# The normalised y of a gated scan block is transposed by DMA instead of TensorE, and its scale and shift go into the gate's weights

## What is computed

```python
y = scan(...)                                        # (B, L, 512)
mu = y.mean(-1, keepdims=True)
var = ((y - mu) ** 2).mean(-1, keepdims=True)
y = (y - mu) * rsqrt(var + LN_EPS) * ln_gamma + ln_beta
gate = sigmoid(y @ W_gate.T + b_gate)
y = gate * y
return concatenate([silu(z0) * x0, y], axis=-1) @ W_out.T
```

## Time and profile before

| what | value |
|---|---|
| time, median of 3 runs (lowest) | 1279.17 us (1274.94) |
| profiled execution: its time, its span | 1281.52 us, 1279.6 us |
| TensorE busy | 1154.4 us (90%) |
| VectorE busy | 994.8 us (78%) |
| ScalarE busy | 960.4 us (75%) |
| GpSimd busy | 393.4 us (31%) |
| mean granted TensorE clock | 0.961 of full speed |
| hardware DMA queue | 32.1% of 16 engines' span |

### The profile page before, as it was taken

One profiled execution on the slowest core, in us unless ns is written; L12 is line 12 of the kernel. 1 busy time (PEld: TensorE's weight loads), 2 busy tenths in 40 slices (PEclk: granted clock), 3 DMA queues, 4 the chain that ended last, 5 costly groups with the idle time before them and its releaser, 6 DMA issues.

```text
span 1279.6 us, 22535 instructions
## 1 busy us (share of the span) xinstructions
PE 1154.4 (90%) x8534; PEld 736.7 (58%) x8534; DVE 994.8 (78%) x1958; ACT 960.4 (75%) x1662; POOL 393.4 (31%) x500
## 2 busy tenths in 40 slices
PE   4577889999999999999999999999998999989885
PEld 1354565647575665657575666656565574747453
DVE  5889786878978798979888897979787696666443
ACT  5847466787979797887879797887877867676744
POOL 1112314152423324142524324252522314232420
PEclk9878899999999999999999999999998999999896
DMA  4720103242423433242423333232253203222443
GB/s 138 202 64 9 34 10 67 34 108 41 94 59 71 80 56 95 42 100 51 92 51 87 71 67 76 51 92 57 52 99 72 54 18 75 50 67 50 82 83 82
DMA packets 238971, 89.10 MB, mean 70 GB/s; under 512 B 207760, under 2 KB 235152, under 8 KB 238864
## 3 DMA queue, kind: packets, MB, share of 16 engines
q1 hardware_dynamic: 238864, 87.67, 32.1%
HBM read 24.32 MB, written 8.39 MB: 26 GB/s over the span
## 4 chain that ended last, share of the span: by engine, by line
PE 59%; ACT 17%; DVE 13%; DMA 5%; issue 4%; POOL 2%; SPq 0%; ACTq 0%; DVEq 0%
PE bank L166 29%; PE bank L140 29%; ACT h L141 3%; ACT L161 3%; DMA hT<-hb 2%; DVE cv L144 2%; DVE EM L144 2%; DVE hb L142 2%; ACT yT L141 2%; ACT hb L141 2%; ACT cv L141 2%; ACT yhl L141 1%; DVE tg L144 1%; POOL caty L142 1%; DVE hn L144 1%
## 5 line engine op out<-in xcount | busy, mean ns | idle before, releaser
L166 PE MATMUL bank<-xnT,win 128*128 128x512 f16 (+1 forms) x1040 | 264.7, 386 | 23.4 <-DMA xnT<-hb 19.1
L144 DVE SCALAR_TENSOR_TENSOR cv<-bank,cws,cv 128x510 f32<-128x510 f32 (+5 forms) x240 | 178.3, 744 | 13.5 <-ACT cv L141 3.0
L166 PE MATMUL bank<-yhl,wg 128*128 128x512 f16 x704 | 169.5, 391 | 10.8 <-DVE yhl L142 10.8
L166 PEld LDWEIGHTS bank<-xnT,win 128*128 128x128 f16 (+1 forms) x1040 | 100.2, 102 | 133.3 <-issue 30.6
L140 PE MATMUL bank<-wpj,hT 128*128 128x256 f16 x1040 | 133.8, 285 | 26.5 <-DMA hT<-hb 23.9
L140 PE MATMUL bank<-wfc,x3T 128*128 128x512 f16 x512 | 132.6, 387 | 8.4 <-DVE dec L145 3.6
L161 ACT ACT_TABLE_LOAD x105 | 134.7, 1283 | 1.9
L140 PEld LDWEIGHTS bank<-wpj,hT 128*128 128x128 f16 x1040 | 103.7, 102 | 53.6 <-ACT hb L141 12.2
L141 ACT ACTIVATE h<-bank,rs 128x512 f32<-128x512 f32 x128 | 87.4, 683 | 62.2 <-PE bank L140 61.2
L166 PEld LDWEIGHTS bank<-yhl,wg 128*128 128x128 f16 x704 | 69.8, 100 | 99.3 <-issue 13.7
L142 POOL TENSOR_TENSOR caty<-tg,caty 128x512 f16<-128x512 f32 x64 | 82.6, 1291 | 114.2 <-ACT caty L141 114.2
(11 more groups left out here) (137 smaller groups left out, 2298.5 us busy)
## 6 DMA issues: line engine op xcount, KB each, us to landing
x<-in_x SPq DMA_DIRECT2D x32, 512.0 KB, 4.2
out_y<-x SPq DMA_DIRECT2D x15, 512.0 KB, 3.0
crep<-cv SPq DMA_DIRECT2D x128, 32.0 KB, 2.0
hT<-hb SPq DMA_TRANSPOSE x128, 3.2
segR<-segL SPq DMA_DIRECT2D x64, 6.0 KB
caty<-in_wg SPq DMA_DIRECT2D x1, 1024.0 KB, 6.0
x<-in_wout SPq DMA_DIRECT2D x1, 1024.0 KB, 9.3
hT<-in_wfc SPq DMA_DIRECT2D x1, 1024.0 KB, 11.4
```

Source lines behind the costliest of these rows:

```text
L144: "scalar_tensor_tensor": lambda e: e.scalar_tensor_tensor(*args, **kw),
L166: self.queue.append(lambda e: e.matmul(*args, **kw))
```

## The change

The task `yout` ends after the normalised chunks are written. A new task `yturn` takes over: for each pair of chunks, `hilo_T` splits the normalised y (tokens on partitions) into hi and lo in the stage `hb0`, and DMA transposes write `yhl` with features on partitions (two per pair, four per block). `yhl` is laid out by chunk. Then for each of the four feature groups POOL adds hi and lo into `yf`, and ACT applies gamma and beta in place. The gate's matmuls read the transposed values without gamma and beta: at the start of the program gamma is multiplied into the gate's weights (four pairs of instructions in place of one), and beta times the weights goes into the gate's bias (16 matmuls of one column). The table PLAN has new figures for all tasks, one more row, and EPS is 0.2.

```diff
--- before.py
+++ after.py
@@ -27,39 +27,39 @@
...
-    "yout": (29.7, 29.6, 47.0, 75.6, 76.1, 75.3, 74.2, 63.8, 65.9, 65.6, 67.1, 68.6, 70.8, 74.1, 74.8, 82.6,
...
+    "yturn": (80.5, 80.2, 80.1, 80.8, 90.7, 90.1, 90.8, 91.9, 94.7, 95.3, 95.6, 96.8, 97.6, 99.9, 98.2, 99.8),
...
-EPS = 0.1
+EPS = 0.2
@@ -217,6 +217,7 @@
         s_k2 = sem("s_k2")
         s_ht = [[sem(f"s_ht{n}{q}") for q in range(2)] for n in range(2)]
         s_xt = [sem(f"s_xt{q}") for q in range(2)]
+        s_y = [sem(f"s_y{q}") for q in range(2)]
         s_x3 = [sem(f"s_x3{q}") for q in range(2)]
         s_seg = [sem(f"s_seg{n}") for n in range(2)]
 
@@ -241,6 +242,7 @@
         lnwb = sb("lnwb", [P, 1024])
         aneg = sb("aneg", [P, 8])
         bgh = sb("bgh", [P, 4])
+        lg64 = sb("lg64", [P, 4])
         cws = sb("cws", [P, 5, 4])
         gam = sb("gam", [P, 4])
         mhalf = sb("mhalf", [P, NCH])
@@ -265,7 +267,7 @@
         ec = sb("ec", [P, T])
         dec = sb("dec", [P, NCH])
         yT = sb("yT", [P, 4, T])
-        yhl = sb("yhl", [P, 2, 4, T], f16)
+        yhl = sb("yhl", [P, 2, NCH, 4, P], f16)
         th = sb("th", [P, T])
         yf = yT
         crest = th[:, 0:P]
@@ -374,7 +376,7 @@
         t_ul = V.do([tu], "tensor_copy", ul[:, :, :], ulf)
         t_cw = V.do([ts], "tensor_scalar", cws[:, :, :], sm("cw").rearrange("p (j k) -> p j k", j=5), 1.0 / SW, None,
                     ALU.mult)
-        t_bg = V.do([ts], "tensor_scalar", bgh[:, :], sm("bg"), 0.5, None, ALU.mult)
+        t_lg = V.do([ts], "tensor_scalar", lg64[:, :], sm("lng"), SW, None, ALU.mult)
 
         def rsqrt(waits, dst, var):
             v = V.do(waits, "tensor_scalar", dst, var, 1e-5, None, ALU.add)
@@ -413,11 +415,24 @@
                     dn["an", 0] = V.do([a], "tensor_scalar", aneg[:, :], aneg[:, :], -1.0, None, ALU.mult)
 
         def prep_gate():
-            yield Need(A, ("twg", 0))
-            a1 = A.do([dn["twg", 0]], "activation", wg[:, 0, :, :], wgs, ACT.Copy, scale=SW)
-            dn["wg", 0] = V.do([a1], "scalar_tensor_tensor", wg[:, 1, :, :].rearrange("p k n -> p (k n)"),
-                               wgs.rearrange("p k n -> p (k n)"), SW, wg[:, 0, :, :].rearrange("p k n -> p (k n)"),
-                               ALU.mult, ALU.subtract)
+
+            yield Need(PE, ("twg", 0), banks=1)
+            b, f = take()
+            PE.wait(f, dn["twg", 0], ts)
+            for g in range(4):
+                for k in range(4):
+                    m = PE.do([], "matmul", b[:, g:g + 1], wgs[:, k, g * P:(g + 1) * P], sm("lnb")[:, k:k + 1],
+                              start=(k == 0), stop=(k == 3))
+            v = V.do([m], "tensor_tensor", bgh[:, :], b[:, 0:4], sm("bg"), ALU.add)
+            give(b, v)
+            dn["bg", 0] = V.do([v], "tensor_scalar", bgh[:, :], bgh[:, :], 0.5, None, ALU.mult)
+            for k in range(4):
+                yield Need(A, ("twg", 0))
+                a1 = A.do([dn["twg", 0], t_lg], "activation", wg[:, 0, k, :], wgs[:, k, :], ACT.Identity,
+                          scale=lg64[:, k:k + 1])
+                v = V.do([a1], "scalar_tensor_tensor", wg[:, 1, k, :], wgs[:, k, :], lg64[:, k:k + 1],
+                         wg[:, 0, k, :], ALU.mult, ALU.subtract)
+            dn["wg", 0] = v
 
         def prep_out():
             for half, s in ((0, SW), (1, SW / 2)):
@@ -492,18 +507,20 @@
                     m = PE.do([], "matmul", b_ap, lhs(p, k), rhs(q, k), start=False, stop=True)
             return m
 
-        def hilo_T(a_waits, src, dst, sems, count, done, war, own=0):
+        def hilo_T(a_waits, src, dst, sems, count, done, war, own=0, grid=None):
 
             stage, hb0, hb1, lock = halves[own], ("hb_free0", own), ("hb_free1", own), f"hb{own}"
             yield Need(A, *a_waits, hb0, *war, lock=lock)
             locked.add(lock)
             ready = [old(*k) for k in war]
-            a = A.do([dn[k] for k in a_waits] + [dn[hb0]], "activation", stage[:, 0, :], src, ACT.Copy)
+            hi, lo = (stage[:, q, :].rearrange("p (c k t) -> p c k t", c=grid[0], k=grid[1]) if grid else stage[:, q, :]
+                      for q in range(2))
+            a = A.do([dn[k] for k in a_waits] + [dn[hb0]], "activation", hi, src, ACT.Copy)
             dn["hb", done] = a
             yield Need(SP, ("hb", done))
             t_hi = SP.dma([a] + ready, sems[0], 16 * count, dst[0], stage[:, 0, :], transpose=True)
             yield Need(V, ("hb", done), hb1)
-            v = V.do([a, dn[hb1]], "tensor_tensor", stage[:, 1, :], src, stage[:, 0, :], ALU.subtract)
+            v = V.do([a, dn[hb1]], "tensor_tensor", lo, src, hi, ALU.subtract)
             dn["split", done] = v
             dn[hb0] = [t_hi, v]
             yield Need(SP, ("split", done))
@@ -836,39 +853,39 @@
                                     b[:, :].rearrange("p (j t) -> p j t", j=4), ACT.Identity, scale=rsy[:, c:c + 1],
                                     bias=nmy[:, c:c + 1])
                 give(b, dn["yn", at])
+
+        def yturn(i):
+
+            for p in range(2):
+                yield from hilo_T([("yn", 4 * i + 2 * p), ("yn", 4 * i + 2 * p + 1)],
+                                  yT[:, :, 2 * p * P:2 * p * P + 2 * P].rearrange("p j (c t) -> p c j t", c=2),
+                                  [yhl[:, q, 2 * p:2 * p + 2, :, :].rearrange("p c k t -> p (c k) t") for q in range(2)],
+                                  s_y, 2 * i + p + 1, ("yhl", 2 * i + p), [("gate_read", i - 1)], grid=(2, 4))
+            dn["y", i] = [dn["yhl", 2 * i], dn["yhl", 2 * i + 1]]
             for j in range(4):
-                yield Need(PE, ("yn", 4 * i + 3), ("gate_read", i - 1), banks=1)
-                b, f = take()
-                PE.wait(f, dn["yn", 4 * i + 3])
-                for c in range(NCH):
-                    m = PE.do([], "transpose", b[:, c * P:(c + 1) * P], yT[:, j, chunk(c)], ident)
-                dn["yt_mm", 4 * i + j] = m
-                yield Need(A, ("yt_mm", 4 * i + j))
-                a = A.do([m], "activation", yf[:, j, :], b[:, :], ACT.Identity,
-                         scale=sm("lng")[:, j:j + 1], bias=sm("lnb")[:, j:j + 1])
-                give(b, a)
-                a = A.do([a, old("gate_read", i - 1)], "activation", yhl[:, 0, j, :], yf[:, j, :], ACT.Copy)
-                dn["yhi", 4 * i + j] = a
-                yield Need(V, ("yhi", 4 * i + j))
-                v = V.do([a, old("gate_read", i - 1)], "tensor_tensor", yhl[:, 1, j, :], yf[:, j, :], yhl[:, 0, j, :],
-                         ALU.subtract)
-            dn["y", i] = v
+                yield Need(G, ("y", i))
+                v = G.do([dn["y", i], dn["split", ("yhl", 2 * i + 1)]], "tensor_tensor",
+                         yf[:, j, :].rearrange("p (c t) -> p c t", c=NCH), yhl[:, 0, :, j, :], yhl[:, 1, :, j, :], ALU.add)
+                dn["ysum", 4 * i + j] = v
+                yield Need(A, ("ysum", 4 * i + j))
+                dn["yf", 4 * i + j] = A.do([v], "activation", yf[:, j, :], yf[:, j, :], ACT.Identity,
+                                           scale=sm("lng")[:, j:j + 1], bias=sm("lnb")[:, j:j + 1])
 
         def gate(i):
             for g in range(4):
                 at = 4 * i + g
                 yield Need(PE, ("y", i), ("wg", 0), ("glo", at - 2), banks=1, func="Tanh")
                 b, f = take()
-                m = three(b[:, :], lambda p, k: wg[:, p, k, g * P:(g + 1) * P], lambda q, k: yhl[:, q, k, :],
+                m = three(b[:, :], lambda p, k: wg[:, p, k, g * P:(g + 1) * P], lambda q, k: yhl[:, q, :, k, :],
                           [f, dn["y", i], dn["wg", 0]], range(4))
                 dn["g_mm", at] = m
                 yield Need(A, ("g_mm", at), func="Tanh")
                 tt = tg[:, g % 2, :]
-                dn["tanh", at] = a = A.do([m, old("glo", at - 2), t_bg], "activation", tt, b[:, :],
+                dn["tanh", at] = a = A.do([m, old("glo", at - 2), dn["bg", 0]], "activation", tt, b[:, :],
                                           ACT.Tanh, scale=0.5 / SW, bias=bgh[:, g:g + 1])
                 give(b, a)
-                yield Need(V, ("tanh", at))
-                dn["yf_read", at] = V.do([a, dn["y", i]], "scalar_tensor_tensor", tt, tt, 1.0, yf[:, g, :],
+                yield Need(V, ("tanh", at), ("yf", at))
+                dn["yf_read", at] = V.do([a, dn["yf", at]], "scalar_tensor_tensor", tt, tt, 1.0, yf[:, g, :],
                                          ALU.add, ALU.mult)
                 yield Need(A, ("yf_read", at), ("cat_read", i - 1), ("wg", 0))
                 a = A.do([dn["yf_read", at], old("cat_read", i - 1)], "activation", caty[:, 0, g, :], tt,
@@ -1002,7 +1019,7 @@
...
+        TASKS = (ln1, conv, silu, dt_chain, inputs, decay, states, mix, yout, yturn, gate, skip, out, turn3, ln3, fc, proj)
```

47 lines of the change are left out of this document (23 added, 24 removed), and 8 rows, old and new, of the table PLAN.

## The result

The changed kernel takes 1305.96 us (median of 4 runs, 1303.72 to 1311.08) beside 1275.97 us for the kernel before in the same comparison: a ratio of 1.0235, 95% interval 1.0191 to 1.0279. (One of the kernel before's four runs took 4025.32 us and is left out; with it the median is 1277.57.) It is slower by 30 us, where 1256 us and a gain of 23.5 us were predicted. The two profiled executions lie closer: their spans are 1301.9 and 1279.6 us, 22.3 us apart, since the profiled one of the changed kernel was its fastest.

What follows compares the result with a forecast made beforehand. TensorE was taken as the main, not only, bound. Savings of 19.3 (TensorE), 2.6 (ACT) and 2.6 (end), less 1.0 (DVE and POOL), made 23.5 us off 1281.5: 1258, or 1256 for the median; range 1230 to 1300.

Steps and rivals of the forecast that it cites:

- The likeliest case: Whole kernel: TensorE is relieved and the rest follows in part; 1256 us, own range 1246 to 1267, chance 0.40.
- DVE and POOL: POOL's 64 new sums slow DVE instructions: net about +5 us for DVE, counted as 1 us, ends 0 and 10.
- rival (c): POOL's sums hold DVE, which becomes the bound and swallows the gain: 1280 us, within 1267 to 1290; chance 0.25.
- TensorE, -19.3 us: Second transposes of y leave TensorE: 28.2 us of work times 0.685 gives 19.3 us saved, ends 0 and 40.
- The 0.685: Share of the middle stretch's chain of waits held by TensorE's two lines, 68.5%, used to scale its relief.
- ACT, the end: ACT's net 20.9 us less work counted as 2.6 us saved; y's shorter path at the run's end, another 2.6.
- The prediction's 2%: A change of 25.6 us, taken as about what a measurement of this kernel can tell from no change.
- The start, 0 to 2 us: Program start: 16 one-column matmuls and four split pairs instead of one, counted as 0, at most 2 us.
- The y path: From a block's last normalised chunk through splits and DMA to complete `yhl`: about 6 us, no new wait counted.
- Rival (d): At the gate TensorE waits for y's DMA transposes, and `hT` behind them is late: slower, 1307 us; chance 0.15.
- Rival (b): `yT`'s life is the true bound and shortens: period under 69 us, 3 us less per block, 1231 us; chance 0.20.
- The clock: A granted clock below 1.00 in the middle stretch would show the forecast wrong from the start; no size given.

Runs made afterwards that it cites:

- its control: The kernel before, all queues in its order, with the residual add of r on 16 columns instead of 512: 1271.12 us, ratio 0.9965.
- without holds: The changed kernel, queues in order, with POOL's sums and residual add on 16 columns and the state update reading PSUM: 1259.72 us, ratio 0.9855.

## Why the prediction was wrong

**The likeliest case comes out only without the change's side effects, and then partly by luck.** With 16-column sums, `S` from PSUM and the late bias the kernel takes 1256.7 us, where 1256 was predicted. But the kernel before took 1275.5 us beside it, so that gain is 18.8 us and not 23.5, and its parts are not those of the sum (below). Put back one after another, the rest of the way is: sums 21.8 (1278.5), bias product early 10.1 (1288.6), `S` from SBUF 17.4 (1306.0), 49.3 us together. The prediction had counted 1 us for the first, at most 2 for the second and nothing for the third.

**DVE and POOL: the step that failed.** It took "The ends are 0 and all 10" and set 1 us; the sums cost 19.5 and 21.8 us. Three things were wrong in it. The amount: it was scaled from how often POOL's present operations hit `EM`. Summed over all DVE instructions, the time above the median of their own shape is 38 us before and 74 after, 36 us more; the sums alone make 29 us of it in both pairs of runs with and without them, 74 to 45 and 64 to 35, and not 10 (all counted from the traces). POOL's present operations follow a conversion on ACT and are spread out; the new ones come four in a row in some blocks, in others the last of them runs into the residual adds, and each DVE instruction with two SBUF tensors that follows waits anew for one of them. The share: 29 us at 7% of the chain is 2 us, and it cost some 20; in the kernel before 20 us more of holds cost 16. So in these three comparisons about two thirds to four fifths of the held time reached the end. The place: rival (c) asked for `EM` well over 0.80, and `EM` fell to 0.758 while `S`, which the prediction did not name, went from 0.351 to 0.665. The four updates of `S` are a chain with TensorE's recurrence directly behind them, and what is lost there is lost once more through TensorE's clock: reading PSUM there took 17.4 us off, nearly as much again as the sums. It is not the only place: with `S` out of PSUM the sums still cost 21.8 us, by holds on `EM`, `tg` and `dtt` above all. The chain of waits told what the present order pays for, not what a new delay at another place would cost.

**Rival (c) had the mechanism** and the rule of the Trainium skill's page "SBUF — State Buffer", at a chance of 0.25, and stopped at 1280 because it let the holds count by a third of DVE's load, and by the sums alone. DVE's busy time rose by 31 us, not by 74, and its share of the middle stretch fell (the earlier trace rows and the row of after). What cost was who waits for the held instructions.

**TensorE, -19.3 us.** The size of the work was right (the transposes' busy time fell from 80.2 to 38.9 us, where its other bound had 40), the share was not a constant: 0 of 21 in the order of before, about a quarter of 28 with the holds, half of it (14.5 us) without them. The 0.685 lay above all of these. That the total still came near rests on gains elsewhere: with its transposes given back and no holds the change is at 1274.3 us, late start of 10 us included, and its control at 1271.1, so ACT, the end and the new order together are worth some 7 us where 5 were counted. They were not taken apart. The prediction's 2% as the least that can be told is also too coarse: the intervals here are 0.1 to 0.5% on either side.

**The start, 0 to 2 us.** The price was looked for in TensorE's idle time, and the order shows the products right ahead of the last block-0 work that the first `yT` needs. 5.47 us of products, most of them at half clock, were 4.8 us of a later start, and moving them took 10 us off in the end.

**The y path** was right: in block 4 the last `yn` ends at 395.7 and the gate starts at 401.76, 6.1 us for the 6 predicted, and TensorE waits 3.3 us in all for `yhl`. Rival (d) was right only in sign: TensorE waits 32.1 us for `hT` instead of 23.9, but it waits 30.6 in the run at 1256.7 as well, so that is not the loss. Rival (b), the open ring, did not come: without holds a period is 70.0 us, not under 69.

**The clock** was named as what would show the forecast wrong from the start, and it did, but no rival had a price for it. Of a long period's 4.6 us extra about 3 are the clock's.

## What to carry over

Before work goes to GpSimd, list the DVE instructions that may be issued while it runs and read how many of their tensors are in SBUF: in all the traces here those that read one from PSUM were never held, the others could be, one after another, through a whole row of GpSimd operations, and the price is set by who waits for the held one, not by DVE's load. Reading one operand from PSUM cost nothing here (348 ns a piece for 351) and took 17 us off the changed kernel. Price a relief of the busiest engine by taking the work out in the present order first; one run would have shown that it is worth nothing there, though in the new order without holds it was worth 14.5 us.
